# Two relational passes of a graph network: gather ring of eight groups instead of four, one-hot tiles made three pairs ahead, four PSUM places for sums, block products one turn later

## The reference, cut to what matters

```
def _rgcn_layer(h, src, dst, et, W, root_w, b, N):
    xw = jnp.einsum('ni,rio->rno', h, W)
    cnt = jnp.zeros((W.shape[0], N), h.dtype).at[et, dst].add(1.0)
    msg = xw[et, src] / cnt[et, dst][:, None]
    agg = jax.ops.segment_sum(msg, dst, num_segments=N)
    return agg + h @ root_w + b
...
for l in range(hop):
    W = jnp.einsum('rb,bio->rio', comp[l], bases[l])
    h = _rgcn_layer(out, src, dst, et, W, root[l], bias[l], N)
    h = jnp.maximum(h, 0.0) if l < hop - 1 else h
    out = SELF_WEIGHT * out + (1.0 - SELF_WEIGHT) * h
```

## Time and profile before

| | |
|---|---|
| median of 3 runs | 5340.59 us (5338.18 to 5340.99) |
| span of the profiled execution | 6547.0 us |
| pass 0, first to last gather of the profiled execution | 2085.5 to 3305.8 us |
| pass 1, the same | 3333.5 to 4537.7 us |
| mean granted TensorE clock | 0.688 |
| busy over the span | PE 3336.5, DVE 2073.9, ACT 964.5, POOL 3039.0 us |

### The profile page before, as it was taken

One profiled execution on the slowest core, in us unless ns is written; L12 is line 12 of the kernel. 1 busy time (PEld: TensorE's weight loads), 2 busy tenths in 40 slices (PEclk: granted clock), 3 DMA queues, 4 the chain that ended last, 5 costly groups with the idle time before them and its releaser, 6 DMA issues. The chain is left out here.

```text
span 6547.0 us, 69273 instructions
## 1 busy us (share of the span) xinstructions
PE 3336.5 (51%) x19582; PEld 2190.3 (33%) x19583; DVE 2073.9 (32%) x6136; ACT 964.5 (15%) x2120; POOL 3039.0 (46%) x3180
## 2 busy tenths in 40 slices
PE   4136553567987333333333333333996455555555
PEld 1013321233444322222223333332443344444444
DVE  5150110114124222222222222223115555555555
ACT  0010000000003000000000000001001455555554
POOL 6645556530001666666656666665000444444442
PEclk7567776778998566666655555555997677777777
DMA  8211110113216222222221111112221122222112
GB/s 230 71 60 40 40 39 20 39 40 119 85 73 175 55 68 63 70 65 67 65 56 45 45 46 45 44 45 75 103 92 46 36 40 40 40 40 40 40 40 53
DMA packets 364319, 408.74 MB, mean 62 GB/s; under 512 B 82995, under 2 KB 298970, under 8 KB 354266
## 3 DMA queue, kind: packets, MB, share of 16 engines
q1 hardware_dynamic: 262746, 295.73, 14.0%
q0 software_dynamic: 101504, 112.13, 8.0%
HBM read 299.63 MB, written 107.98 MB: 62 GB/s over the span
## 5 line engine op out<-in xcount | busy, mean ns | idle before, releaser
L653 POOL DMA_INDIRECT GS<-xw_table,stage x1664 | 1572.7, 945 | 1550.6 <-issue 1177.5
L1147 PE MATMUL psum<-HA,HT 128*128 128x512 fp8e4 (+1 forms) x5733 | 1245.5, 378 | 201.0 <-DVE HT L1793 148.2
L653 POOL DMA_INDIRECT HA<-p_table,stage x676 | 641.8, 949 | 1279.1 <-ACT stage L928 551.5
L687 POOL DMA_INDIRECT adj<-cell_value,cell_i x832 | 817.7, 983 | 595.5 <-issue 244.5
L1099 PE MATMUL psum<-GS 128*128 128x96 f32 x3328 | 684.7, 381 | 639.6 <-DMA GS<-xw_table,stage 556.6
L1099 PEld LDWEIGHTS psum<-GS 128*128 128x128 f32 x3328 | 632.4, 287 | 688.5 <-issue 685.3
L1147 PEld LDWEIGHTS psum<-HA,HT 128*128 128x128 bf16 x5733 | 552.6, 100 | 867.7 <-issue 149.5
L1610 DVE TENSOR_SCALAR GS<-iota,HT,wt 128x96 f32<-128x96 f32 x1680 | 472.0, 349 | 451.0 <-issue 448.7
L1624 DVE TENSOR_TENSOR HA<-HA,psum 128x96 f32 x208 | 52.9, 254 | 1387.7 <-remote 1029.7
L1078 PE MATMUL psum<-Wcat,HT 128*128 128x512 f32 x196 | 180.2, 1073 | 484.3 <-DVE HT L2089 454.9
L1878 DVE SCALAR_TENSOR_TENSOR GS<-psum,keep,O 128x512 f32<-128x512 f32 (+1 forms) x26 | 18.7, 720 | 1221.9 <-PE psum L1167 903.3
(11 more groups left out here) (350 smaller groups left out, 3627.3 us busy)
## 6 DMA issues: line engine op xcount, KB each, us to landing
HA<-adj SPq DMA_DIRECT2D x39, 1600.0 KB
HA<-adj SPq DMA_DIRECT2D x39, 1536.0 KB
HT<-dst_rows SPq DMA_DIRECT2D x212, 256.0 KB
xw_table<-HT SPq DMA_DIRECT2D x100, 512.0 KB, 3.2
adj<-O SPq DMA_DIRECT2D x13, 3136.0 KB, 18.4
GS<-xw_table,stage POOLq DMA_INDIRECT x1664
adj<-cell_value,cell_i POOLq DMA_INDIRECT x832
HA<-p_table,stage POOLq DMA_INDIRECT x676
```

What stands on the lines that cost most here:

```text
L653: nc.gpsimd.indirect_dma_start(out=to, out_offset=None, in_=table, in_offset=bass.IndirectOffsetOnAxis(ap=idx, axis=0)).then_inc(done, 16)
L687: nc.gpsimd.indirect_dma_start(out=adj, out_offset=bass.IndirectOffsetOnAxis(ap=cell_i[:, t:t + 1], axis=0), in_=cell_value[:, t:t + 1].bi ...
L1147: last = nc.tensor.matmul(bank[s][:, 0:w], Hs4[:, b, t, :], adj_tile[s][:, b * GW:b * GW + w], start=(b == 0 and t == 0), stop=(b == SRCS ...
```

## The change

The same arithmetic is done in the same number of instructions in the loops, with more room between the engines:

- the ring of gathered groups has eight places in place of four: the four of `G3` and four in `H`; `gathered` has eight semaphores, and GpSimd's wait looks back two turns (`CREDIT` 8 for 4);
- `windows` runs `AHEAD` = 3 pairs ahead of the sum in place of 1, in four buffers (now in `T`); three pairs are made before the first turn of a pass, the loop on VectorE, PE has a body of two turns;
- the sums of four successive pairs go to banks 0, 1, 5 and 7, so `sums_added` starts at 4;
- ScalarE stages a turn's row numbers after the gathers of two turns before have landed, where it waited for PE's sums;
- blocks are combined `LAG` = 6 turns later in place of 5, and their products, copies and stores, or their transposes and additions, `PRODUCT_LAG` = 7 turns later; `hop_sum` has two places. Banks 2 to 4, bank 6 and `xw_out[0]` stay single. After the last turn three blocks are left to combine (they were two) and four to multiply and store, or to turn and add (they were two);
- some turns at the start of a pass are written out ahead of the loops.

```
-LAG = 5
+LAG = 6
+PRODUCT_LAG = 7
+AHEAD = 3
...
-CREDIT = 4
+CREDIT = 8
...
+        S_pair = [T[:, 2048 + i * 2 * GT * WINDOW:2048 + (i + 1) * 2 * GT * WINDOW].rearrange("p (j d) -> p j d", d=WINDOW) for i in range(4)]
+        ring = G3 + [H[:, g * GT * P:(g + 1) * GT * P].rearrange("p (j f) -> p j f", f=P) for g in range(4)]
...
+        hop_sum = [tail[:, 1024:1024 + P], H[:, 4 * GT * P:4 * GT * P + P]]
+        pair_sums = [bank[i][:, 0:WINDOW] for i in (0, 1, 5, 7)]
...
-                sp.wait_ge(hop_evac_d, b + 2)
+                sp.wait_ge(hop_evac_d, b + 3)
...
-                                gather(G3[g][:, j, 0:P], table, stage16[u][:, t:t + 1], gathered[g])
+                                gather(ring[u * 4 + g][:, j, 0:P], table, stage16[u][:, t:t + 1], gathered[u * 4 + g])
...
-                    act.wait_ge(windows_summed, GROUPS * l + it * 4)
+                    for g in range(4):
+                        act.wait_ge(gathered[u * 4 + g], 64 * (ITERS // 2 * l + round_before))
...
+                def iterations(i2, with_blocks):
+                    for u in range(2):
+                        for h in range(2):
+                            q = u * 2 + h
+                            k = i2 * 4 + q
+                            pe.wait_ge(windows_ready, (PAIRS + AHEAD) * l + k + 1)
+                            pe.wait_ge(sums_added, PAIRS * l + k + 1)
+                            for g in (2 * h, 2 * h + 1):
+                                pe.wait_ge(gathered[u * 4 + g], 64 * (ITERS // 2 * l + i2 + 1))
...
+                            if h == 0 and u in with_blocks:
+                                of_block(i2 * 2 + u - PRODUCT_LAG, 1 - u)
...
+                for b in range(PRODUCTS_IN_PASS, HOP_BLOCKS):
+                    of_block(b, b % 2)
...
+                if l == 0:
+                    for place in (2, 3):
+                        dve.wait_ge(xw_stored[place], 16 * stores_at(place))
+                for k in range(AHEAD):
+                    windows(k, k)
...
+                            windows(k + AHEAD, (q + AHEAD) % 4)
+                            dve.wait_ge(windows_summed, GROUPS * l + 2 * k + 2 + CREDIT)
+                            dve.wait_ge(sums_added, PAIRS * l + k + 4)
+                            to = A[:, bass.ds(at[q], WINDOW)]
+                            V.tensor_tensor(to, to, pair_sums[q], ALU.add).then_inc(sums_added, 1)
+                            if h == 0 and combining:
+                                combine(i2 * 2 + u - LAG, u)
+                            if h == 1 and u in with_evacuation:
+                                evacuate(i2 * 2 + u - PRODUCT_LAG, 1 - u)
...
                 for b in range(IN_PASS, HOP_BLOCKS):
-                    for step in beside:
-                        step(b)
+                    combine(b, b % 2)
+                    evacuate(b - 1, (b - 1) % 2)
+                evacuate(HOP_BLOCKS - 1, (HOP_BLOCKS - 1) % 2)
```

More of the change, by code:

```diff
@@ L327, in gnn_stack @@
         pool_turn = sem("pool_turn")
-        gathered = [sem(f"gathered{g}") for g in range(4)]
+        gathered = [sem(f"gathered{g}") for g in range(8)]
         windows_ready = sem("windows_ready")
@@ L761, in stage_pass, with iteration @@
             def stage_pass(l):
[L763 removed]
+                def iteration(i2, u, last=False):
+                    it = i2 * 2 + u
                     if not last:
[L765 to L767 removed]
+                        stage_columns(l, it + 1, 1 - u, i2 + u)
+                    if l == 0 and not is_block(it, *range(PRODUCT_LAG)):
+                        evacuate_next(it - PRODUCT_LAG)
                 stage_columns(l, 0, 0)
[L770 to L772 removed]
+                for it in range(PRODUCT_LAG + 1):
+                    iteration(it // 2, it % 2)
+                with act.Fori((PRODUCT_LAG + 1) // 2, ITERS // 2 - 1) as i2:
                     for u in range(2):
[L774 to L776 removed]
+                        iteration(i2, u)
+                iteration(ITERS // 2 - 1, 0)
+                iteration(ITERS // 2 - 1, 1, last=True)
                 if l == 0:
[L778 removed]
+                    for b in range(PRODUCTS_IN_PASS, HOP_BLOCKS):
                         evacuate_next(b)
@@ L1087, in sum_pass @@
             def sum_pass(l, of_block):
[L1089 to L1110, removed]
+                def iterations(i2, with_blocks):
[7 more added lines that the diff above has]
+                                pe.wait_ge(gathered[u * 4 + g], 64 * (ITERS // 2 * l + i2 + 1))
+                                pe.sem_inc(pe_turn, 1)
+                                for j in range(GT):
+                                    t = (g % 2) * GT + j
+                                    last = nc.tensor.matmul(pair_sums[q], ring[u * 4 + g][:, j, :], S_pair[q][:, t, :],
+                                                            start=(t == 0), stop=(t == 2 * GT - 1))
+                                last.then_inc(windows_summed, 1)
+                            if h == 0 and u in with_blocks:
+                                of_block(i2 * 2 + u - PRODUCT_LAG, 1 - u)
@@ L1112, in rest_pass @@
+                with pe.Fori(0, PRODUCT_LAG // 2) as i2:
+                    iterations(i2, ())
+                iterations(PRODUCT_LAG // 2, (1,))
+                with pe.Fori(PRODUCT_LAG // 2 + 1, ITERS // 2) as i2:
+                    iterations(i2, (0, 1))
+                for b in range(PRODUCTS_IN_PASS, HOP_BLOCKS):
+                    of_block(b, b % 2)
             def rest_pass(z):
@@ L1604, in _, with sum_pass @@
             over_half = lambda t: t.unsqueeze(1).broadcast_to([P, NB // 2, P])
-            def sum_pass(l, beside):
+            def sum_pass(l, combine, evacuate):
                 def windows(k, s):
@@ L1612, in windows @@
                     last.then_inc(windows_ready, 1)
[L1614 to L1632, removed]
+                if l == 0:
[3 more added lines that the diff above has]
+                    windows(k, k)
+                def iterations(i2, with_evacuation, combining=True):
+                    at = [dve.value_load(pair_i[0:1, bass.ds(i2 * 4 + q, 1)], min_val=0, max_val=TRASH_COL) for q in range(4)]
+                    for u in range(2):
+                        for h in range(2):
+                            q = u * 2 + h
+                            k = i2 * 4 + q
+                            windows(k + AHEAD, (q + AHEAD) % 4)
[7 more added lines that the diff above has]
+                                evacuate(i2 * 2 + u - PRODUCT_LAG, 1 - u)
```

49 lines of the change are left out of this document (27 added, 22 removed).

## The result

The changed kernel takes 5354.6 us (median of 9 runs, 5353.1 to 5356.28); the kernel before takes 5340.99 us (9 runs). The ratio is 1.0026 with a 95% interval of 1.0017 to 1.0034: 13.6 us slower, the interval reaching from +9 to +18 us. The forecast was 5350.6 us with a range of 5275 to 5360.

A forecast was written before the change was run, and what follows sets the result against it. The prediction took POOL's (GpSimd's) issuing of gathers to bound both passes in a timed run. Loop changes at 0, pass 0's end +8.7 and pass 1's end +1.3 us gave 5340.6 + 10.0 = 5350.6 us, range 5275 to 5360.

The forecast's parts named there:

- GpSimd's issuing bounds the passes: Both passes: gathers issue 1.25 us apart, 831 steps make 1038.8 us, and a timed run keeps 0 us of standstill.
- The slack: Ring of four groups: a buffer is wanted after 20.0 us and summed after 13.4 us, so 6.6 us to spare.
- The tail of pass 0: End of pass 0: four blocks, 18.2 us, follow the last turn instead of two, 9.50 us; cost +8.7 us (+7.9 to +9.6).
- The tail of pass 1: End of pass 1: four blocks of about 1.1 us, 4.4 us, instead of two in 3.09 us; cost +1.3 us.
- The standstill belongs to the recorder: Both passes: GpSimd's 347 us of standing still in the profiled execution come from recording and are absent from timed runs.
- late news: In the passes, PE's finished sums reach waiting engines late; VectorE added one 16.2 us after it was over.
- subtraction: Of the profile's extra 1206.4 us, other stages can give 1033, so timed passes keep at most 174 us of standstill.
- the two statements: On the recorder's block: it holds producers back, which would throttle an engine; no overflow was seen at 6.6 million notes a second.
- The forecast of 6380 us for the profiled span: Changed kernel's profiled execution: 32 gathers between stops instead of 16 halve the 347 us; 6547 - 174 + 10.
- The tail costs more: Rival, chance 0.30: each of pass 0's four blocks costs 5.16 us, pass 1's end +3.1 us; 5354.8 us.
- Part: Rival, chance 0.15: timed passes have 45 us of real standstill, which the change removes; 5306 us.
- bulk of the standstill is real: Rival, chance 0.08: all 347 us of standstill in the passes are in timed runs and go; 5004 us.

The follow-up runs named there:

- the short lag: The changed kernel with LAG 4 and PRODUCT_LAG 5 in place of 6 and 7; 5344.5 us, 1.0007 of the kernel before, without the standstill.

## Why the prediction came out as it did

**GpSimd's issuing bounds the passes: right.** The passes took 1038.6 and 1038.3 us against 1038.8; a quarter of the gathers less gave 521.6 us against 520, half of the matmuls nothing. The slack that the prediction had worked out for four groups, 6.6 us, was there and larger: 20.0 - 9.0 = 11.0 us for the group at 2299.81 above. The edits inside the loops leave the passes at their length, as taken. It is why the ring of eight could not help.

**The tail of pass 0: right in mechanism, 0.5 to 1.4 us too small.** 18.70 us were measured where 18.2 had been summed. The terms: 4.77 and 4.34 us for the two kinds of block were 4.64 and 4.72, and 4.43 and 4.91. The last one is off: it is ended by the landing of the store before it, which took 3.7 us where the stores of the two blocks before took 3.2. Another 0.86 us was not in the sum at all, from the last copy to the first gather: 6.97 against 6.11 us; the last store lands after 4.0 us. In the run of half of the matmuls the stores land within 3.2 to 3.5 us. This isn't chance: the other profiled execution of the changed kernel has a last block of 4.89 us (3310.81 to 3315.70) and 7.0 us behind it (to 3322.7). The changed kernel with the short lag has 6.53 us there. Why these stores land later is open. By the traces the tail costs 18.70 - 9.81 + 0.86 = +9.8 us, where +8.7 was forecast.

**The tail of pass 1: +0.6 us where +1.3 was forecast.** A block takes 0.92 us, not 1.1.

Sum by the traces: +10.4 us, forecast +10.0, measured +13.6 with +9 to +18 as its interval. That the two sums agree so well is partly luck: one tail was 1.1 us too small and the other 0.7 us too large, and the assumption of two blocks of each kind, carried over from one of each in the earlier trace rows, came true here, while in the run of the short lag both blocks had PE's lower level. About 3 us are assigned to nothing, and the interval doesn't require that there be anything. The traces can't settle it: the first gather of pass 0 alone starts anywhere from 1786.7 to 1790.2 us in the four profiled executions without standstill that keep all gathers.

**The standstill belongs to the recorder: this step fell.** The prediction asked whether late news was in the timed runs, and answered by subtraction that it came with the recording. But the profiled executions of the third occasion and of the result have none (5353.2 us, and 5341.5 for the run of half of the matmuls), while on chips 13 and 9 each of the 62 executions of the kernel before took 6464 to 6563 us. The profiled execution even stands among the nine runs of the result, with 5355.06 us, and a span (5351.2 to 5354.4 us) is on record for each of the nine. So what is ahead of the prediction, that the runs of the median were taken without the recorder and that this makes the 1206.4 us, isn't borne out. What fits the runs is that the profiled execution of before, at 6547.0 us, was made under the condition of chips 13 and 9, and its median was not; that execution's own chip isn't on record. The recording alone, at 69,053 instructions, held nothing back. This is all that the runs say on the two statements weighed there from the Trainium skill (NOTIFIC — the notification-queue block, section 7.1, Overflow); no row shows the block itself. That no overflow was ever seen doesn't say that nothing was held back, so the second statement couldn't decide between the two readings. Whether the recording takes part in the standstill where there is one isn't excluded.

The number survived since its second leg, the slack, didn't need the cause. The subtraction was loose but sound as a bound: by the kernel after, scatters lost 283 of the 328 us that it allowed them (39.6 to 1131.7 against the earlier trace rows), attention 533 of 539 (4449.6 to 5299.6 against the earlier trace rows), the passes all of the 347. It had allowed the passes up to 174 us in a timed run and taken 0; 0 was right. The forecast of 6380 us for the profiled span rested on the same wrong step. Its second assumption, that a ring of eight halves the standstill, is wrong too: 324 to 333 us stayed where there was one.

**The rivals.** *The tail costs more* gave 5354.8 us, and the time came to 5354.6, but not on its way: a block averaged 4.68 us, if only just under the 4.72 from which it decides, and pass 1's end was cheap. Where PE stayed at its lower level, in the run of the short lag, blocks did take 5.14 and 5.33 us, as this rival has it. *Part* and *bulk of the standstill is real* are refuted where the standstill is absent, and where it is present they fail as well, because the change doesn't remove it.

## What to carry to other kernels

Work out the pace of the engine that issues, and compare the loop's length with count times pace before adding buffers: where they agree, depth inside the loop is worth nothing, and a longer lag costs one serial block for each turn of lag at every point where the pipeline must drain. Shorten the drain instead: one turn less of lag, and the copy ahead of a wait that it doesn't need, together gave 6 us here (interval 2 to 12). And when a profiled execution is 20% off the median, run the same kernel again on another occasion before explaining the difference.

## What the runs showed of the hardware

The kernel before takes 5341 us on some occasions (one of them on chip 1) and 6478 and 6537 us on others (chips 9 and 13); every variant that was run there changes with it. Where it takes the longer time, while GpSimd issues gathers, PE and VectorE get instructions one by one for part of each turn, as PE's at 2641.67, 2643.07 and 2644.47 above, 1.40 us apart, or VectorE's in the earlier trace rows; gathers themselves keep 1.25 us. A pass takes 1183 to 1228 us there, 22.8 to 23.6 us a turn, with two, four or eight groups in the ring, against 20.0 us. What causes it stays open: a kernel with fewer instructions, for one, wasn't tried under it.
